# Delta rule on Trainium2: keys multiply the state inside the recurrence, with projections and Gram products between its steps

## The chip, the cores and the metric

The kernel runs on one core of a Trainium2 chip (trn2). TensorE (PE) multiplies, VectorE (DVE) and ScalarE (ACT) work on tiles, GpSimd (POOL) fills tiles, SyncE (SP) issues the transfers. The metric is the device time in microseconds of one execution; less is better. All data is fp32.

## The reference, cut to what matters

The kernel computes four stages in a row: a gated mixer, a mixture of experts, a gated delta rule and an attention over selected tokens. The change is in the third. For every element (B = 8 sequences of T = 512 tokens, H = 8 heads, keys of 128, values of 64) the reference walks the tokens with a state of 64 x 128 for each head:

```python
q, k, v = conv_silu(x @ Wq), conv_silu(x @ Wk), conv_silu(x @ Wv)
q, k = l2norm(q), l2norm(k)
def step(state, inp):
    q_t, k_t, v_t, a_t, b_t = inp
    retained = einsum('bhvk,bhk->bhv', state, k_t)
    state = a_t * (state - b_t * outer(retained, k_t)) + b_t * outer(v_t, k_t)
    return state, einsum('bhvk,bhk->bhv', state, q_t)
out = out * rsqrt(mean(out ** 2) + 1e-5) * o_norm_w * silu(x @ Wg)
y = x + out.reshape(T, 512) @ Wo
```

## The kernel before, in words

`stage_delta` treats the 512 tokens of an element in NC = 4 chunks of 128. Inside a chunk the walk over tokens becomes the inverse of a triangular 128 x 128 matrix for each head, so that all is matrix products, and only the state goes from chunk to chunk (the recurrence).

For an element b, PE does in this order (names of the code in brackets): 8 key projections (`proj`, L1378); the recurrence of the element before it, pb (`scan`, L1392 to L1411); for each chunk the Gram products keys x keys (`gram_kk`, L1422); 4 value projections; the key transposes (`k_transposes`, L1431); 8 query and 4 gate projections; the output transposes and output projection of pb (`project_out`, L1442, L1447); the inversion of b's blocks from 32 to 64 to 128 rows (`invert`: L1463, L1469, L1480, L1485, L1492 for two chunks, then for the other two); at the end of each of the two halves of `invert` the products of scaled keys with the inverse (L1500), which give WT, "the keys already multiplied"; then in `tail` the value transposes (L1509), the products keys x queries (L1518) and the query norms (products with a column of ones, L1523).

In `scan` each chunk has five groups of 8 head products: XT x values and, added in the same bank, WT x state, which give U; queries x state; keys x decayed U, which gives the next state (not for the last chunk); PQ x U, the output. DVE and ACT stand between them: ACT copies U (`u`, L1592), DVE decays state and U (L1743, L1747), adds the new state (L1752) and the output (L1756, L1761). Between these DVE does the causal convolutions (`conv`, three operations each, L1735) and the decay scans (L1765). After the Gram products DVE multiplies them by the decays (L1812), then computes the output's norm (L1816 to L1826) and applies it and the gate (L1828, L1830: semaphore `yf`), then inverts the 32 x 32 diagonal blocks of b by substitution (L1838 to L1858), then adds the residual (L1863, semaphore `outr`), for which `invert` waits. In `invert` DVE scales what PE produced (L1872, L1880) between the convolutions of values and queries.

Every engine runs its own program in a fixed order and waits on semaphores. The first element and the last recurrence are written out, the seven steps between are a hardware loop:

```python
body(None, 0)
with pe.Fori(0, BATCH - 1) as pb:
    body(pb, pb + 1)
body(BATCH - 1, None)
```

## Time and profile before

| | us |
|---|---|
| median of 3 runs (3804.80 to 3806.32) | 3805.78 |
| the profiled execution | 3808.81 |
| its span, first to last instruction | 3806.2 |
| mean granted TensorE clock | 0.864 |

The page gives each engine's busy share over all four stages, so it says little on one of them. The delta rule stage is read from the timeline (instructions of one engine in order of time, merged where they repeat, with the idle time before them and what ended it) and from the busy time by stretch, which also gives the clock that was granted to TensorE: 1.00 is 2.4 GHz and 0.50 is 1.2 GHz, and a value between is a stretch that saw both. A matmul's end is modelled: the start of the next instruction is the safer mark.

### The profile page before, as it was taken

Reading aid. Unit: us, or ns where it says so; the run is one execution under the profiler, and the core shown is the slowest. Engines: PE = TensorE matmul, PEld = TensorE weight load, DVE = VectorE, ACT = ScalarE, POOL = GpSimd, SP = SyncE. Lnnn points to the kernel's source line nnn. Section 1 sums busy time; section 2 is a strip of 40 time slices with the busy share of each in tenths; the row PEclk is TensorE's granted clock in tenths of the full one; section 3 lists DMA queues with packets and bytes.
Section 4 is the critical chain, followed back from the end, with each engine's and each line's share of the span. In section 5 each row is a group of like instructions: output and inputs, shape, how many; then the busy total and the mean of one; then the engine's idle time right before and its main releaser. Section 6 shows DMA issues by size and latency. Waiting matters only on the chain. (4 is left out here: it accounts for less than half of the span.)

```text
span 3806.2 us, 52445 instructions
## 1 busy us (share of the span) xinstructions
PE 3262.9 (86%) x18666; PEld 2525.1 (66%) x18666; DVE 2396.6 (63%) x5801; ACT 1356.5 (36%) x2713; POOL 158.4 (4%) x158
## 2 busy tenths in 40 slices
PE   5999938888999999747989898989898989488887
PEld 2665524445999999714867686868686869355554
DVE  6788425554777777766685858576767673354542
ACT  2333202221444444314534444444444442033232
POOL 0000000015111111000000000000000000000000
PEclk8999958999999999968797988888888886588786
DMA  1000080022899989741011111110111100100000
GB/s 62 23 17 12 11 160 12 11 75 81 305 322 317 320 318 323 253 152 64 34 34 35 34 36 34 35 34 35 34 35 34 35 20 1 53 12 23 12 17 12
DMA packets 203686, 327.31 MB, mean 86 GB/s; under 512 B 37449, under 2 KB 157522, under 8 KB 202258
## 3 DMA queue, kind: packets, MB, share of 16 engines
q1 hardware_dynamic: 196930, 305.94, 24.4%
q0 software_dynamic: 6480, 17.77, 1.2%
q8 instruction: 164, 2.69, 0.3%
q14 instruction: 112, 0.92, 0.1%
HBM read 275.15 MB, written 48.50 MB: 85 GB/s over the span
## 5 line engine op out<-in xcount | busy, mean ns | idle before, releaser
L767 PE MATMUL ex_ps<-ex_xbT,ex_w 128*128 128x128 f32 x4544 | 531.2, 275 | 1.7 <-DMA ex_b<-in_b_all_dram 1.2
L767 PEld LDWEIGHTS ex_ps<-ex_xbT,ex_w 128*128 128x128 f32 x4544 | 524.3, 192 | 6.1 <-DMA ex_b<-in_b_all_dram 1.8
L1378 PE MATMUL de_ps<-de_hT,de_w 128*128 128x512 f32 x640 | 306.2, 636 | 27.6 <-DMA de_w<-in_w_kqv_dram 13.9
L896 ACT ACTIVATE ex_t<-ex_ps,ex_b 128x128 f32<-128x128 f32 x568 | 208.8, 368 | 337.0 <-PE ex_ps L767 319.1
L1378 PEld LDWEIGHTS de_ps<-de_hT,de_w 128*128 128x128 f32 x640 | 129.0, 207 | 188.1 <-issue 186.0
L711 PE MATMUL ex_ps<-ex_xT,ex_w 128*128 128x512 f32 x512 | 230.6, 607 | 12.5 <-DVE ex_gl L1008 9.1
L1008 DVE SCALAR_TENSOR_TENSOR ex_gl<-ex_ps,ex_b,ex_t 128x128 f32<-128x128 f32 (+1 forms) x316 | 123.7, 391 | 137.3 <-ACT ex_t L896 69.4
L711 PEld LDWEIGHTS ex_ps<-ex_xT,ex_w 128*128 128x128 f32 x512 | 98.0, 195 | 131.8 <-issue 115.0
L1735 DVE SCALAR_TENSOR_TENSOR de_ya<-de_kx,de_taps,de_ya 128x512 f32<-128x512 f32 x192 | 142.5, 751 | 49.2 <-ACT de_ya L1574 44.7
L1008 DVE SCALAR_TENSOR_TENSOR ex_gm<-ex_ps,ex_b,ex_t 128x128 f32<-128x128 f32 (+1 forms) x316 | 121.8, 385 | 48.9 <-ACT ex_t L869 46.6
L177 PE MATMUL mx_ps<-mx_hT,mx_w_in 128*128 128x512 f32 x320 | 143.6, 605 | 8.3 <-ACT mx_hT L249 8.3
L1735 DVE SCALAR_TENSOR_TENSOR de_ya<-de_qx,de_taps,de_ya 128x512 f32<-128x512 f32 x192 | 142.9, 751 | 8.7 <-ACT de_ya L1574 2.6
L779 PE MATMUL ex_ps<-ex_w,ex_hid 128*128 128x256 f32 x568 | 134.5, 380 | 1.8 <-DVE ex_hid L1033 1.8
L1485 PE MATMUL de_ps<-de_PQ,de_DG 64*128 64x64 f32 x512 | 113.4, 419 | 15.7 <-ACT de_PQ L1638 15.7
L1485 PEld LDWEIGHTS de_ps<-de_PQ,de_DG 64*128 64x128 f32 x512 | 110.4, 329 | 19.6 <-ACT de_PQ L1638 19.6
L869 ACT ACTIVATE ex_t<-ex_ps,ex_b 128x512 f32<-128x512 f32 x64 | 44.0, 687 | 207.3 <-PE ex_ps L711 207.3
L177 PEld LDWEIGHTS mx_ps<-mx_hT,mx_w_in 128*128 128x128 f32 x320 | 60.7, 193 | 81.6 <-issue 67.4
L211 PE MATMUL mx_ps<-mx_h2T,mx_w_fc 128*128 128x512 f32 x256 | 113.7, 603 | 0.8 <-ACT mx_h2T L271 0.8
L1030 DVE SCALAR_TENSOR_TENSOR ex_gl<-ex_gl,ex_gm 128x128 f32<-128x128 f32 (+1 forms) x316 | 105.4, 333 | 11.1 <-DVE ex_gl L1028 0.2
L1033 DVE TENSOR_TENSOR ex_hid<-ex_gl,ex_gs 128x128 f32<-128x128 f32 (+1 forms) x316 | 105.0, 332 | 11.2 <-DVE ex_gl L1030 0.2
L220 PE MATMUL mx_ps<-mx_w_proj,mx_hid 128*128 128x256 f32 x512 | 111.8, 379 | 0.0
L779 PEld LDWEIGHTS ex_ps<-ex_w,ex_hid 128*128 128x128 f32 x568 | 102.5, 190 | 12.9 <-DVE ex_hid L1033 1.9
(378 smaller groups left out, 6268.3 us busy)
## 6 DMA issues: line engine op xcount, KB each, us to landing
ex_w<-in_w_all_dram SPq DMA_DIRECT2D x144, 1024.0 KB, 6.5
ex_w<-in_w_all_dram SPq DMA_DIRECT2D x72, 512.0 KB, 8.6
de_w<-in_w_kqv_dram SPq DMA_DIRECT2D x80, 256.0 KB, 2.8
de_ab<-alpha_d SPq DMA_DIRECT2D x8, 2048.0 KB, 8.3
ex_xb<-ex_xs_d SPq DMA_DIRECT2D x71, 129.0 KB
ex_xs_d<-ex_blank SPq DMA_DIRECT2D x71, 128.5 KB, 8.3
ex_w<-ex_y_d SPq DMA_DIRECT2D x16, 512.0 KB, 6.1
mx_xin<-in_x_dram SPq DMA_DIRECT2D x8, 512.0 KB, 4.0
```

The source lines that it names most:

```text
L177: m = pe.matmul(ps[:, (n + 2) % 4, :], w_in[:, k, part * DIM + half * P:part * DIM + (half + 1) * P], hT[:, k, :], start=(k == 0), stop=(k ...
L211: m = pe.matmul(ps[:, 4 + f % 2, :], w_fc[:, k, f * P:(f + 1) * P], h2T[:, k, :], start=(k == 0), stop=(k == KT - 1))
L220: m = pe.matmul(ps[:, 6 + t // 2, t % 2 * DIM:(t % 2 + 1) * DIM], hid[:, f, t * P:(t + 1) * P], w_proj[:, f, :], start=(f == 0), stop=(f = ...
L711: m = pe.matmul(ps[:, bank, :], w[:, k, part * HID + c * P:part * HID + (c + 1) * P], xT[:, i % (LAG + 1), k, :], start=(k == 0), stop=(k ...
L767: m = pe.matmul(ps[:, n % 4, x * BLK:(x + 1) * BLK], w[:, k, part * HID + c * P:part * HID + (c + 1) * P], xbT[sx][:, k, :], start=(k == 0 ...
L779: m = pe.matmul(ps[:, 4 + sx, t * DIM:(t + 1) * DIM], hid[:, sx, c, t * P:(t + 1) * P], w2[s][:, c, :], start=(c == 0), stop=(c == HT - 1))
L896: act.activation(t1[:, n % 2, 0:BLK], ps[:, n % 4, 0:BLK], ACT.Identity, bias=b13[s][:, 0, n:n + 1]).then_inc(t1_ready, 1)
L1008: dve.scalar_tensor_tensor(out=out[:, 0:width], in0=in0, scalar=b3[:, 1, n:n + 1], in1=t1[:, n % 2, 0:width], op0=ALU.add, op1=ALU.mult).t ...
L1030: link2(dve.scalar_tensor_tensor(out=gl[:, 0:width], in0=gl[:, 0:width], scalar=1.0, in1=gm[:, 0:width], op0=ALU.add, op1=ALU.mult))
L1378: m = pe.matmul(ps[:, n % 2, :], w[:, g % SLOTS, k, n % 2 * P:(n % 2 + 1) * P], hT[:, k, :], start=(k == 0), stop=(k == KT - 1))
L1485: m = pe.matmul(ps[:, 2 + c % 2, hd * HALF:(hd + 1) * HALF], DG[0:HALF, c, hd, :], X11[0:HALF, c % 2, hd, :], start=True, stop=True, skip_ ...
L1735: m = dve.scalar_tensor_tensor(out=ya[:, n % 3, :], in0=xp(n)[:, i:i + SEQ], scalar=taps[:, col_of(n), i:i + 1], in1=ya[:, n % 3, :], op0= ...
```

## The change

`WT` and its products (L1500) are gone, with ACT's scalings of the keys (L1614) and copies of the result (L1646). In the recurrence the convolved keys multiply the state (`with_state`), DVE scales that and adds it to the values (`add_state`), and only then XT multiplies the sum (`u_products`). For the first chunk, whose state is zero, there are no products with the state: `first_state` and `first_out` are copies. The 4 value projections and the 4 Gram groups of b stand between the steps of pb's recurrence. The keys have two buffers, so that b's can be projected while pb's are used. The squares of the output go from DVE to ACT, the query norm to the start of DVE's part, the loop is written out (`for pb, b in steps`), the residual is loaded into the output tile once that has been transposed, and `Xc` shares the value tile, so that POOL fills it with zeros for each element.

```diff
         PQ = sb("PQ", [P, NC, H, C])
...
         Y5 = sb("Y5", [P, 2, H, HALF])
         tmp = th[:, 0, :]
...
+        squared = lambda t: spare[:, (1 + t // 2 * 2) * Q * Q + t % 2 * VD:(1 + t // 2 * 2) * Q * Q + (t % 2 + 1) * VD]
...
-            def scan(pb):
...
-                pe.wait_ge(s["wt"], pb * NC + NC)
-                for c in range(NC):
-                    bank = 2 + c % 2
+            def scan(pb, b):
+                def u_products(c):
                     for hd in range(H):
-                        pe.matmul(ps[:, bank, hd * V:(hd + 1) * V], XT[:, c, hd, :], vb[:, c, hd, :],
-                                  start=(hd == 0), stop=False, skip_group_check=True)
-                    pe.wait_ge(s["st"], pb * NC + c + 1)
+                        m = pe.matmul(ps[:, 2, hd * V:(hd + 1) * V], XT[:, c, hd, :], vb[:, c, hd, :], start=True, stop=True, skip_group_check=True)
+                    m.then_inc(s["up"], 1)
...
+                def with_state(c):
...
-                        m = pe.matmul(ps[:, bank, hd * V:(hd + 1) * V], WT[:, c, hd, :], ST[:, hd, :],
-                                      start=False, stop=True, skip_group_check=True)
-                    m.then_inc(s["up"], 1)
-                    if c:
-                        pe.wait_ge(s["od"], pb * NC + c)
+                        m = pe.matmul(ps[:, 3, hd * V:(hd + 1) * V], kc(pb, hd, c), ST[:, hd, :], start=True, stop=True, skip_group_check=True)
+                    m.then_inc(s["ks"], 1)
...
-                    if c < NC - 1:
...
+                    pe.wait_ge(s["vs"], pb * (NC - 1) + c)
+
+                def state_step(c):
+                    pe.wait_ge(s["ud"], pb * (NC - 1) + c + 1)
+                    for hd in range(H):
+                        m = pe.matmul(ps[:, 3, hd * V:(hd + 1) * V], kt[:, c, hd, :], Ud[:, hd, :], start=True, stop=True, skip_group_check=True)
+                    m.then_inc(s["su"], 1)
+
...
+                pe.wait_ge(s["pq"], pb * NC + NC)
+                pe.wait_ge(s["vbr"], pb * NC + NC)
+                u_products(0)
+                value(0)
+                state_step(0), outputs(0)
+                value(1)
+                with_state(1), u_products(1)
+                value(2)
+                state_step(1), outputs(1)
+                value(3)
+                with_state(2), u_products(2)
+                if b is not None:
+                    gram_kk(pb, b, 0)
+                state_step(2), outputs(2)
+                if b is not None:
+                    gram_kk(pb, b, 1)
+                with_state(3), u_products(3)
+                if b is not None:
+                    gram_kk(pb, b, 2)
+                outputs(3)
+                if b is not None:
+                    gram_kk(pb, b, 3)
...
-                    pe.wait_ge(s["dg"], b * NC + min(NC, c + 3))
...
                         if p:
-                            pe.wait_ge(s["wt"], b * NC + 2)
+                            pe.wait_ge(s["y6"], b * NC + c - 1)
...
-                    for c in both:
-                        pe.wait_ge(s["x6"], b * NC + c + 1)
-                        pe.wait_ge(s["kcg"], b * NC + c + 1)
-                        bank = 6 if c % 2 == 0 else 2
-                        for hd in range(H):
-                            m = pe.matmul(wide(bank)[:, hd, :], kcg[:, c % 2, hd, :], XT[:, c, hd, :], start=True, stop=True, skip_group_check=True)
-                        m.then_inc(s["wp"], 1)
...
-                pe.wait_ge(s["wt"], b * NC + NC)
                 pe.wait_ge(s["vbr"], b * NC + NC)
+                pe.wait_ge(s["x6"], b * NC + NC)
...
-                    scan(pb)
-                if b is not None:
-                    gram_kk(pb, b)
+                    scan(pb, b)
+                else:
                     for n in range(V0, Q0):
-                        proj(b, n, pb is None)
-                    k_transposes(b)
+                        proj(b, n, True)
+                    for c in range(NC):
+                        gram_kk(None, b, c)
+                if b is not None:
+                    k_transposes(pb, b)
...
-                    step(2, 7), step(3, 7), step(4, 7)
-                u(0)
-                if b is not None:
-                    step(5, 7), step(6, 7)
-                u(1)
-                if b is not None:
-                    step(7, 7)
-                u(2), u(3)
-                if b is not None:
-                    cp(8), cp(9)
+                    step(2, 7), step(3, 7), step(4, 7), step(5, 7)
+                    u(0)
+                    cp(8)
+                    step(6, 7), step(7, 7)
+                    cp(9)
+                    u(1)
+                    cp(10), cp(11)
+                    tap(8), tap(9)
+                    u(2)
+                    squares(0), squares(1)
                     diagonals(0)
-                    cp(10), cp(11)
+                    u(3)
+                    squares(2), squares(3)
                     diagonals(1)
-                    tap(8), tap(9)
                     for c in range(NC):
                         k_out(c)
                     for n in range(Q0, PROJ):
                         cp(n)
-                        if n == 15:
-                            scaled_k(0)
-                    scaled_k(1)
...
-                        step(n + 3, CONV - 1)
-                        w_out(2 * p), w_out(2 * p + 1)
-                        step(n + 4, CONV - 1)
-                        if p == 0:
-                            scaled_k(2)
-                        step(n + 5, CONV - 1)
-                        if p == 0:
-                            scaled_k(3)
+                        step(n + 3, CONV - 1), step(n + 4, CONV - 1), step(n + 5, CONV - 1)
...
+            for pb, b in steps:
+                body(pb, b)
...
+            for b in range(BATCH):
+                if b:
+                    pool.wait_ge(s["up"], (b - 1) * NC + NC)
+                pool.memset(Xc, 0.0).then_inc(s["xz"], 1)
...
+                def first_state():
+                    dve.wait_ge(s["su"], pb * (NC - 1) + 1)
+                    dve.tensor_copy(ST, heads(3)).then_inc(s["st"], 1)
...
+                def add_state(c):
+                    dve.wait_ge(s["ks"], pb * (NC - 1) + c)
+                    dve.wait_ge(s["scl"], pb + 1)
+                    cB(dve.tensor_tensor(KV[:, :, :], heads(3), over_v(ncg[:, pb % 2, c, :]), ALU.mult))
+                    dve.tensor_tensor(vb[:, c, :, :], vb[:, c, :, :], KV[:, :, :], ALU.add).then_inc(s["vs"], 1)
...
+                def first_out():
+                    if pb:
+                        dve.wait_ge(s["out_st"], 16 * pb)
+                    dve.wait_ge(s["os"], pb * NC + 1)
+                    dve.tensor_copy(o[:, 0, :, :], heads(5)).then_inc(s["od"], 1)
...
-                    dve.memset(ST, 0.0).then_inc(s["st"], 1)
...
-                        cD(dve.tensor_tensor(oT[:, t, :].rearrange("p (h v) -> p h v", v=V), o[:, t, :, :], o[:, t, :, :], ALU.mult))
-                        cD(dve.tensor_reduce(om[:, t, :], oT[:, t, :].rearrange("p (h v) -> p h v", v=V), AX.X, ALU.add), wait=(t == TT - 1))
+
+                def sum_squares(t):
+                    dve.wait_ge(s["sqo"], pb * TT + t + 1)
+                    cD(dve.tensor_reduce(om[:, t, :], squared(t).rearrange("p (h v) -> p h v", v=V), AX.X, ALU.add), wait=(t == TT - 1))
...
+                        query_norm()
+                        for n in range(6):
+                            conv(n)
+                        dve.wait_ge(s["cl_ld"], 32 * pb + 32)
+                        decay_u(0)
+                        conv(6)
+                        first_state()
+                        conv(7)
+                        first_out()
+                        decay_state(1)
+                        dve.wait_ge(s["ab_ld"], 16 * b + 16)
+                        decay(0, 1)
+                        add_state(1)
+                        decay(1, 2)
+                        out_a(1)
+                        decay_u(1)
+                        decay(2, 4)
+                        new_state(1)
+                        decay(4, 5)
+                        out_b(1)
+                        decay_state(2)
+                        decay(5, 6)
+                        add_state(2)
+                        decay(6, 7)
+                        out_a(2)
+                        decay_u(2)
+                        decay(7, H)
+                        decayed_gram(0)
+                        new_state(2)
+                        out_b(2)
+                        sum_squares(0), sum_squares(1)
+                        decayed_gram(1)
+                        add_state(3)
+                        out_a(3)
+                        decayed_gram(2)
+                        out_b(3)
+                        cB.end()
+                        decayed_gram(3)
+                        sum_squares(2), sum_squares(3)
+                        normalise()
+
```

## Rows read from the trace of the kernel before

**Rows 1.** The page: busy time, share of the span and instructions of each engine.
```profile
PE 3262.9 (86%) x18666; PEld 2525.1 (66%) x18666; DVE 2396.6 (63%) x5801; ACT 1356.5 (36%) x2713; POOL 158.4 (4%) x158
```

**Rows 2.** Busy time by stretch: length; PE, PEld, DVE, ACT, POOL busy; clock; DMA share; GB/s.
```profile
1985.00:3115.00 1130.00, 1018.07 (x6240) 832.38 (x6240) 788.44 (x1447) 499.13 (x902) 0.00 (x0) 0.85 0.11 35
```

**Rows 3.** Timeline of PE: start, length in us, line, tiles, count [idle before <-releaser].
```profile
1713.16 12.78 PE L1378 MATMUL de_ps<-de_hT,de_w 128*128 128x512 f32 x24 [13.94 <-DMA de_w<-in_w_kqv_dram]
1801.27 7.06 PE L1463 MATMUL de_ps<-de_Xc,de_DG 128*128 128x64 f32 x32 [7.77 <-ACT de_Xc L1620]
1876.90 13.98 PE L1378 MATMUL de_ps<-de_hT,de_w 128*128 128x512 f32 x32
2063.53 6.95 PE L1378 MATMUL de_ps<-de_hT,de_w 128*128 128x512 f32 x9 [1.87 <-issue]
2178.24 3.78 PE L1463 MATMUL de_ps<-de_Xc,de_DG 128*128 128x64 f32 x32 [1.63 <-DVE de_xin L1863]
2197.84 5.98 PE L1500 MATMUL de_ps<-de_XT,de_kcg 128*128 128x128 f32 x32
2204.93 3.79 PE L1463 MATMUL de_ps<-de_Xc,de_DG 128*128 128x64 f32 x32 [1.11 <-ACT de_DG L1646]
2234.81 2.02 PE L1518 MATMUL de_ps<-de_qx,de_kx 128*128 128x128 f32 x16 [0.87 <-DVE de_vb L1892]
2250.99 16.96 PE L1378 MATMUL de_ps<-de_hT,de_w 128*128 128x512 f32 x32 [1.75 <-issue]
2303.36 7.38 PE L1422 MATMUL de_ps<-de_kx 128*128 128x128 f32 x64 [0.96 <-DVE de_o L1761]
2323.32 3.65 PE L1431 MATMUL de_ps<-de_ident,de_kx 128*128 128x128 f32 x16 [3.97 <-ACT de_kt L1596]
3187.74 2.69 PE L1392 MATMUL de_ps<-de_vb,de_XT 128*128 128x64 f32 x16
```

**Rows 4.** Timeline of DVE, same columns.
```profile
2124.32 0.17 DVE L1816 TENSOR_SCALAR de_th<-de_nq 128x32 f32<-128x32 f32 x1
2132.61 0.19 DVE L1822 TENSOR_TENSOR de_th<-de_th 128x32 f32<-128x32 f32 x1
2140.93 2.12 DVE L1838 STREAM_TRANSPOSE de_PQ<-de_PQ 128x1024 f32<-128x1024 f32 x1
2176.75 1.22 DVE L1863 TENSOR_TENSOR de_xin<-de_xin,de_ps 128x1024 f32<-128x1024 f32 x1 [1.54 <-PE de_ps L1447]
2223.02 6.96 DVE L1735 SCALAR_TENSOR_TENSOR de_ya<-de_qx,de_taps,de_ya 128x512 f32<-128x512 f32 x9
2273.19 2.32 DVE L1735 SCALAR_TENSOR_TENSOR de_ya<-de_kx,de_taps,de_ya 128x512 f32<-128x512 f32 x3
3282.88 1.22 DVE L1863 TENSOR_TENSOR de_xin<-de_xin,de_ps 128x1024 f32<-128x1024 f32 x1 [13.55 <-PE de_ps L1447]
```

**Rows 5.** Busy time by stretch: length, PE busy (instructions), granted clock, DMA share, GB/s.
```profile
1741.40:1745.00 3.60, 3.52 (x16) 0.50 0.00 0
1745.00:1748.70 3.70, 1.97 (x18) 1.00 0.00 0
1801.20:1814.60 13.40, 12.58 (x80) 0.50 0.01 1
1814.60:1825.20 10.60, 10.59 (x64) 0.50 0.01 2
1832.60:1839.00 6.40, 5.84 (x64) 1.00 0.00 0
2234.80:2249.30 14.50, 14.42 (x128) 1.00 0.01 2
2267.80:2303.30 35.50, 34.46 (x305) 1.00 0.03 9
3190.30:3251.90 61.60, 61.58 (x289) 0.50 0.00 1
3251.90:3269.40 17.50, 0.01 (x1) 0.50 0.00 0
```

## What I expect of the change, before seeing it run

> **What bounds the kernel now.** I read the page first: TensorE is busy for 86% of 3806.2 us [rows 1], but the page averages four stages. The busy time by stretch puts the middle of the delta rule stage at 1130 us with PE busy for 1018 and the granted clock at 0.85 [rows 2]. So I laid that stage out by the timeline of PE, then of DVE. The stage runs from the first key projection at 1713.2 us to the last residual addition at 3284.1 (1571 us). It has one opening part, 1713.2 to 1876.9 (163.7 us), seven middle steps, 1876.9 to 3187.7 (1310.8 us, 187.3 each), in each of which the recurrence of one element meets the projections and inversion of the next, and a last part of 96.4 us [rows 3, 4].
>
> One middle step, counted from its first key projection, has three stretches [rows 3]. A: projections, recurrence, Gram products, output projection, up to the first product of the inversion (2063.53 to 2178.24, 114.7 us). B: inversion, up to the first key-query product (2178.24 to 2234.81, 56.6). C: key-query and norm products and the loop's branch (2234.81 to 2250.99, 16.2). Two facts decide what the change is worth.
>
> First, A is PE's only up to the Gram products. Then DVE takes over: the output's normalisation ends at 2141.0, at once the inversion of the diagonal blocks runs until 2175.2, the residual is added at 2176.75 (behind 1.54 of waiting), and only then PE may start L1463 [rows 3, 4]. PE's work on the way has slack against this.
>
> Second, the clock. PE runs at 1.00 (2.4 GHz) or 0.50 (1.2 GHz). In the opening part it started L1463 at 0.50 after an idle time of 7.77 us [rows 3], stayed at 0.50 through L1463, L1469, L1480, L1485 and L1492 (24.0 us), and came back only behind the dense 128 x 128 x 128 products of L1500 [rows 5]. After L1500 the products of C run at 1.00. In the last part there is no projection before the recurrence: the 64-column groups run at 0.50 for 61.6 us and never bring the clock back, though PE has no pause [rows 5]. In the middle steps the same groups run at 1.00 behind the projections [rows 5].
>
> **The change part by part.** I lay one middle step out anew, t = 0 at its first key projection.
>
> Loop gone. Six of seven steps now start behind a branch: PE waits 1.75 to 1.87 us with no releaser but issue, and the eight key projections take 16.8 us to the next group's start where the unrolled entry took 13.8 (16.96 and 13.98 in the rows) [rows 3]. Straight code takes the 1.75 away in every step. The other 3.0 is the low clock, and it stays if C ends at 0.50; I keep 16.8 (bounds 13.8 to 16.8).
>
> Recurrence. Per step 19 groups of 16 products become 17 (the state's first two products and the second XT-side product pair are gone for chunk 0; WT x state becomes keys x state). A group costs 34.46 / 19 = 1.8 us, and PE waited for 1.0 in the whole stretch [rows 5]. Four value projections of 13.8 / 8 = 1.72 and four Gram groups of 1.8 move in between, and were on PE's path before, so they cost nothing new. New is a wait: PE does U(0) and one value projection, 16.8 + 3.5 = 20.3, and then needs the decayed U, which DVE now issues behind conv(5). In the old timeline conv(5) starts two 0.6 us operations later than it now can, at 2273.19, and takes 2.3 [rows 4]: 2250.99 + 24.0 is when the new one lands. PE idles 3.8 us. An idle time of 3.97 us stands before the second half of the key transposes, which then take 3.65 us, that is half clock [rows 3]; so two 64-column groups and part of a value projection run low: 3.2 us more, bounds 0 and 5.0. The new pair on DVE that scales keys x state and adds it (two operations of 0.69) is covered by the query group of 1.79 that PE runs meanwhile; if one decay scan of 1.1 is ahead of it, up to 1.1 shows, three times. I take 0. The rest of PE's line is 16 groups, 3 projections and 4 Gram groups: 28.8 + 5.2 + 7.2 = 41.2. The last Gram group ends at 24.1 + 41.2 + 3.2 = 68.5. Before, it started at 2303.36 and ran 7.2 us [rows 3], so it ended 59.6 us into the step.
>
> Normalisation. The 13 small operations on the query norm (from 2124.32, 0.2 us each and their gaps, some 2.9) move to the start, where DVE waits for taps, and the four squares move to ACT, beside PE's groups. Behind the last Gram group remain 0.3 + 1.1 (decayed Gram), 1.2 (two reductions) and 8.4 (2132.61 to 2140.93 and a little) [rows 4]: ready at 79.5. Before it was 77.5. So what left DVE is used up by the Gram products coming 8.9 later. Inversion 34.3 and addition 1.2 follow: L1463 may start at 115.1. Stretch A: 114.7 before, 115.1 after. The queue entries moved here are SP's load of the residual (behind the output transposes, 3.9 us to land, needed 15 us later; SP only has the store behind it) and POOL's fill of the shared Xc tile (after the last U, some 45 us before it is used): nothing. ACT's four value copies now stand between the U copies and are 0.6 each; nothing.
>
> PE meanwhile ends the output projection near 107, some 7 us before 115.1, as in the opening part. So B starts at 0.50.
>
> Inversion. The 64 dense products of L1500 per element are gone (5.98 us in the first half [rows 3], about as much in the second, and 1.1 of waiting between them and the next half's start at 2204.9: 12.8 in all) as are ACT's 32 scalings and 4 copies. But with L1500 goes what brought the clock back. Two halves of 24.0 us at 0.50 lie end to end: 48.0 [rows 5]. DVE ends later: its last three convolutions (7.0) follow the second Y6 at 45.3, end at 52.1, and the value transposes and scalings with their hand-overs take 3.7. First key-query product at 56.0. Stretch B: 56.6 before, 56.0 after. The 12.8 us taken out buy 0.6.
>
> Stretch C. Nothing in it is changed, yet it now begins at 0.50. Its eight groups (four of 128-column products, four of one-column ones, each bound by loading its weights) took 14.5 us at 1.00 [rows 5]. At 0.50 sixteen such products take 3.41 us, as the 289 in 61.6 us of the last part show [rows 5]: 27.3. Stretch C: 16.2 before, 27.3 after.
>
> Sum: 115.1 + 56.0 + 27.3 = 198.4 per step; seven give 1388.8 against 1310.8, so +78.0. The opening part loses 12.8 us of L1500 and up to 7.8 of waiting (the diagonal copies no longer stand behind value copies on ACT) and pays 13 in C: I take 0, bounds -13 and +3. The last part: two groups at 0.50 less (-6.8), 17.5 us of idle PE [rows 5] become 10.6, and new hand-overs with nothing between (U to its decay, 1.0 each, four times) cost 4.1, with the output products slower: about -8. In all +70. The profiled execution took 3808.8 us, its span 3806.2; it becomes 3879. The median of the runs lies 3.0 below the profiled one, so 3876.
>
> A rule that bears on the recurrence: the Trainium skill, "TensorE: Matmul & The Clock Gate", section "A second HAM failure mode: psum-queue depth-cycling", says that many short idle times between groups of products make the clock swing between its two levels. The old recurrence, with waits below 1.1 us between groups, ran at 1.00 throughout, so this trace doesn't bear it out for short waits. Taken at its word it is the third rival.
>
> **Rivals.** (1) The clock comes back in C. Its first key-query group is as dense as L1500's, and two such groups, the Gram products at 1741, began at 0.50 and were followed by 1.00 [rows 5]; against it, each dense group is followed by an equal time of one-column products, and nothing in the trace shows this mix started at 0.50. If it returns behind the first group, C takes 3.4 + 12.6 = 16.0 and the next projections 13.8: the step is 115.1 - 3.0 + 56.0 + 16.0 = 184.1, seven save 22, the opening part 11, the last 8: 3765, or up to 3795 where it fails in two or three steps. This is the case on the other side, faster; it decides on where in C the clock turns.
> (2) It comes back in every second or third step only: 3 to 4 steps at 184 to 188, the rest at 198: 3815 to 3845.
> (3) The low clock after the 3.8 us wait stays through the recurrence, as it did in the last part. Then some 20 groups more run at 0.50, 34 us in each such step. For it speaks that 64-column groups don't lift it; against it the value projection of full width that stands third. One such step gives 3909, two to five 3940 to 4050.
> (4) The change doesn't do what it says: the clock behaves in B as before although PE idled 7 us. Then B keeps 44 to 56, C 14.5, and a step is 170 to 183: 3670 to 3755. The opening part speaks against it.
> (5) Gains and losses cancel, 3798 to 3813: a mixture of (1) and (2).
>
> **How the numbers follow.** Forecast, including one step of (3) at most: 3850 to 3915, chance 0.47. (1) and (4) 0.12, (2) 0.14, (3) with more steps 0.22, (5) 0.05. The range takes in the forecast, (2), (5), the dearer edge of (1), and (3) up to two steps: 3795 to 3955. Within 0.2% (7.6 us, about what a measurement of this kernel can tell from no change) only (5) falls: 0.05. Faster 0.12, slower 0.83.
>
> **What would show it.** Right: PE idle for 3 to 4 us before the first keys x U group of each step; the gap before the first inversion product near 7 us; the granted clock at 0.50 from there through L1492 of both halves; the key-query stretch at 27 us; steps of 198. Wrong: a key-query stretch at 1.00, an inversion that starts earlier than 112 us into the step, or a recurrence at 1.00 throughout.

## The result, and the profile after

The changed kernel takes 3837.39 us (median of 4 runs, 3835.62 to 3847.45) against 3805.29 for the kernel before in the same comparison: a ratio of 1.0091, 95% interval 1.0073 to 1.0109. It is slower by 32 us. I had forecast +70 (3876), so the direction was right and the size was more than twice the real one. The profiled execution spans 3836.0 us, 29.8 more than the one of before.

The busy times of the page move little, against [rows 1]: PE lost 768 instructions and is still busy 30 us longer, and ACT lost 84 us of work.

```profile
PE 3293.1 (86%) x17898; PEld 2559.0 (67%) x17898; DVE 2394.9 (62%) x5793; ACT 1272.0 (33%) x2457; POOL 171.1 (4%) x165
```

Where the 29.8 us come from is seen when each step is a stretch of its own. The columns are those of [rows 2]: length; PE, PEld, DVE, ACT, POOL busy; clock; DMA share; GB/s. The first row is the opening part (without its first 1.3 us), the others the seven middle steps.

```profile
1713.00:1865.50 152.50, 125.91 (x623) 95.68 (x623) 103.19 (x177) 66.66 (x107) 0.00 (x0) 0.74 0.09 32
1865.50:2050.10 184.60, 164.79 (x946) 135.45 (x945) 131.20 (x240) 72.33 (x118) 1.80 (x1) 0.80 0.11 35
2050.20:2234.60 184.40, 164.62 (x946) 135.61 (x946) 131.13 (x240) 72.33 (x118) 1.80 (x1) 0.80 0.11 35
2234.60:2430.80 196.20, 176.33 (x947) 147.34 (x946) 131.20 (x240) 72.33 (x118) 1.80 (x1) 0.75 0.11 35
2430.80:2629.50 198.70, 178.68 (x945) 148.39 (x946) 131.21 (x240) 72.32 (x118) 1.80 (x1) 0.73 0.10 33
2629.50:2827.60 198.10, 178.05 (x945) 148.22 (x946) 131.15 (x240) 72.33 (x118) 1.80 (x1) 0.73 0.10 33
2827.60:3025.70 198.10, 177.99 (x946) 148.19 (x946) 131.19 (x240) 72.33 (x118) 1.80 (x1) 0.73 0.10 33
3025.70:3223.70 198.00, 177.87 (x946) 148.11 (x946) 131.19 (x240) 72.32 (x118) 1.80 (x1) 0.73 0.07 25
```

All seven steps hold the same work (945 to 947 matmul instructions, the same DVE and ACT time to 0.1 us), yet there are two lengths. The last four take the forecast's 198 us. The first two take 184.5, and the third lies between. Against the 187.3 us of before, the seven together cost +47.3 (1358.2 against 1310.8). The opening part, 153.8 us from its first projection against 163.7 [rows 3], gives back 9.9. The last part, from 3223.7 to the last residual addition at 3313.1, gives back 6.9. The stage begins 1.5 earlier, and what follows it takes 0.8 longer: in all +29.8.

What separates the two lengths is the clock of the key-query stretch. The timeline of PE (columns of [rows 3]) for the third element and then for the fourth, each from the second pair of value transposes on:

```profile
2216.14 1.97 PE L1531 MATMUL de_ps<-de_ident,de_vx 128*128 128x128 f32 x8 [3.00 <-DVE de_vb L1952]
2218.94 3.40 PE L1540 MATMUL de_ps<-de_qx,de_kx 128*128 128x128 f32 x16 [0.83 <-issue]
2222.17 1.84 PE L1545 MATMUL de_ps<-de_ones,de_ya 128*128 128x1 f32 x16
2223.88 2.03 PE L1540 MATMUL de_ps<-de_qx,de_kx 128*128 128x128 f32 x16
...
2234.60 13.98 PE L1376 MATMUL de_ps<-de_hT,de_w 128*128 128x512 f32 x32
```

```profile
2400.67 1.97 PE L1531 MATMUL de_ps<-de_ident,de_vx 128*128 128x128 f32 x8 [3.00 <-DVE de_vb L1952]
2403.47 3.75 PE L1540 MATMUL de_ps<-de_qx,de_kx 128*128 128x128 f32 x16 [0.83 <-issue]
2407.01 3.41 PE L1545 MATMUL de_ps<-de_ones,de_ya 128*128 128x1 f32 x16
2410.29 3.76 PE L1540 MATMUL de_ps<-de_qx,de_kx 128*128 128x128 f32 x16
...
2430.77 17.00 PE L1376 MATMUL de_ps<-de_hT,de_w 128*128 128x512 f32 x32
```

Both come out of the inversion at 0.50, with the same pauses of 3.00 and 0.83 us, and their first key-query group begins at 0.50. In the upper one the clock turns near that group's end: the next group takes 1.84, and so on at 1.00. In the lower one it doesn't: the whole stretch runs at 0.50, and so do the first 6 us of the next projections (0.51 from 2430.8 to 2437.0, then 1.00), which take 17.00 instead of 13.98. By stretch:

```profile
2219.00:2234.60 15.60, 15.60 (x129) 15.60 (x129) 4.90 (x4) 3.15 (x5) 0.00 (x0) 0.91 0.01 1
2403.50:2430.80 27.30, 27.30 (x129) 27.30 (x129) 4.90 (x4) 3.15 (x5) 0.00 (x0) 0.50 0.04 10
```

The first three of the eight stretches came back (16.0, 15.7 and 15.6 us), the other five took 27.3 each. The rest of a step is as it was laid out:

```profile
2255.59 3.37 PE L1403 MATMUL de_ps<-de_oT,de_kt 128*128 128x64 f32 x16 [3.51 <-DVE de_oT L1760]
2258.76 3.62 PE L1409 MATMUL de_ps<-de_oT,de_PQ 128*128 128x64 f32 x16
2262.17 3.73 PE L1376 MATMUL de_ps<-de_hT,de_w 128*128 128x512 f32 x4
2265.69 2.14 PE L1392 MATMUL de_ps<-de_oT,de_kx 128*128 128x64 f32 x16
...
2347.75 7.06 PE L1492 MATMUL de_ps<-de_vb,de_DG 128*128 128x64 f32 x32 [6.70 <-DVE de_o L1921]
```

```profile
2347.80:2371.70 23.90, 23.08 (x144) 22.33 (x144) 12.45 (x19) 10.21 (x17) 0.00 (x0) 0.50 0.25 80
2371.70:2395.70 24.00, 23.18 (x146) 22.41 (x145) 16.45 (x25) 10.97 (x20) 0.00 (x0) 0.50 0.00 1
```

The wait for the decayed U is there (3.51), two groups and the value projection behind it run at 0.50 and then the clock is back, PE is idle 6.70 us before the inversion, and the two inversion halves take 24 us each at 0.50 throughout. Before, the second half was followed by dense products at L1500 and the key-query products ran at 1.00 [rows 3, 5].

### The profile page after: what moved, and what is told of

Read it like the earlier page. It is cut to its first block and busy times, and to the rows that moved or that the text cites. A ratio compares the mean times of both kernels' runs of the same rounds, so it can differ in the third digit from the quotient of the medians.

```text
span 3836.0 us, 48336 instructions
## 1 busy us (share of the span) xinstructions
PE 3293.1 (86%) x17898; PEld 2559.0 (67%) x17898; DVE 2394.9 (62%) x5793; ACT 1272.0 (33%) x2457; POOL 171.1 (4%) x165
## 5 line engine op out<-in xcount | busy, mean ns | idle before, releaser
L1376 PE MATMUL de_ps<-de_hT,de_w 128*128 128x512 f32 x640 | 312.0, 642 | 19.2 <-DMA de_w<-in_w_kqv_dram 13.8
L1492 PE MATMUL de_ps<-de_vb,de_DG 128*128 128x64 f32 x512 | 113.2, 422 | 56.9 <-DVE de_o L1921 47.6
L1492 PEld LDWEIGHTS de_ps<-de_vb,de_DG 128*128 128x128 f32 x512 | 110.4, 332 | 61.2 <-issue 60.3
L1956 DVE TENSOR_TENSOR de_PQ<-de_ps,de_ab 128x1024 f32<-128x1024 f32 x32 | 39.2, 1225 | 135.0 <-PE de_ps L1540 135.0
```

The costliest lines, as they stand in the source:

```text
L1376: m = pe.matmul(ps[:, n % 2, :], w[:, g % SLOTS, k, n % 2 * P:(n % 2 + 1) * P], hT[:, k, :], start=(k == 0), stop=(k == KT - 1))
L1492: m = pe.matmul(ps[:, 2 + c % 2, hd * HALF:(hd + 1) * HALF], DG[:, c, hd, :], Xc[:, c * H + hd, :], start=True, stop=True, skip_group_chec ...
```

## The experiments

The theory: all that the change takes away, and more, goes to the clock. The dense products of L1500 had brought it back. Without them only the first key-query group can, and whether it does hangs on the moment at which it falls. The rivals: something the first elements do differently, the waits of the new order, or the loop.

**1. The old kernel, its loop written out.** It isolates the loop, the part of the change that has nothing to do with the order of work.

```diff
...
-            body(None, 0)
-            with pe.Fori(0, BATCH - 1) as pb:
-                body(pb, pb + 1)
-            body(BATCH - 1, None)
+            for pb, b in steps:
+                body(pb, b)
```

> The kernel before with its hardware loop written out, nothing else. In the kernel before, six of its seven middle steps begin with 1.75 to 1.87 us of idle PE and with a clock at 0.50 for the first projections (16.8 us for eight instead of 13.8); the one step that is written out takes 186.6 by 13.8. Theory (the branch costs its idle time, and through that idle time the clock at the start of the next step): 4.7 to 6.3 us per step for six steps, so 3768 to 3778. Rival (a step's length is set by DVE's chain, and what PE gains at the start is waited for later): 3795 to 3806.

Measured: 3783.39, ratio 0.9931 (0.9915 to 0.9948): 26 us faster than the kernel before in this comparison (3809.43), 22 against the 3805.29 above. The idle time and the slow projections are both gone (the eight take 13.98 again), so the price of the branch is real. But six steps became 184.3 to 184.4, not 181 to 183; one took 180.8. The first inversion half tells why. It takes 26.7 us in the old kernel's loop [rows 3] and 30.5 here:

```profile
2537.65 6.51 PE L1462 MATMUL de_ps<-de_Xc,de_DG 128*128 128x64 f32 x32 [3.29 <-DVE de_xin L1858]
2544.09 3.62 PE L1468 MATMUL de_ps<-de_PQ,de_Y 128*64 128x32 f32 x32
```

PE arrives earlier, waits 3.29 us instead of 1.63 [rows 3], and enters the inversion with the clock falling. Part of what straight code gave at the front was paid back there. The change therefore has to be held against 3783, and its new order of work costs some 54 us, not 32 (58 if each is held against the kernel before in its own comparison, 52 by the spans of the two traces).

**2. The old kernel with thin products at L1500.** Same count, place and waits; only 32 of the 128 rows are contracted. (The timeline counts each of these fp32 products twice: a group of eight in the code is x16. L1500 has four such groups per element: 32 products in the code, 64 in the timeline. The text below speaks of 64 groups and means these.)

```diff
-                            m = pe.matmul(wide(bank)[:, hd, :], kcg[:, c % 2, hd, :], XT[:, c, hd, :], start=True, stop=True, skip_group_check=True)
+                            m = pe.matmul(wide(bank)[:, hd, :], kcg[0:Q, c % 2, hd, :], XT[0:Q, c, hd, :], start=True, stop=True, skip_group_check=True)
```

> The kernel before with its 64 groups of products at L1500 contracted over 32 of the 128 rows (the result of these products is therefore not the reference's). Their count, their place and all waits stay. Theory (the dense products of L1500 brought the clock back to 1.00 for what follows, and that is what the change lost): the first half's L1500 no longer brings 1.00, the second half of the inversion and the key-query products run at 0.50, a step takes 12 to 16 us more than 187.3, the kernel 3880 to 3915. Rival (the clock comes back by the key-query products or the transposes in any case, and L1500 is only time): within 5 us of 3806, and key-query products at 1.00.

Measured: 3896.54, 87 us slower, as the theory said. L1500 and what follows it, in the third middle step:

```profile
2409.76 6.82 PE L1500 MATMUL de_ps<-de_XT,de_kcg 32*128 32x128 f32 x31
2417.68 7.09 PE L1463 MATMUL de_ps<-de_Xc,de_DG 128*128 128x64 f32 x32 [1.11 <-ACT de_DG L1646]
```

In the old kernel these rows are 5.98 and 3.79 us [rows 3]. The second inversion half ran at 0.50 in all eight elements, and three of the eight key-query stretches stayed at 0.50 from end to end; the other five came back, without a pattern that their work explains. In four of these five the clock was back before the key-query products began, behind the value transposes, which follow the thin products without a pause:

```profile
1864.78 3.50 PE L1509 MATMUL de_ps<-de_ident,de_vx 128*128 128x128 f32 x16
1869.26 2.02 PE L1518 MATMUL de_ps<-de_qx,de_kx 128*128 128x128 f32 x16 [0.98 <-DVE de_vb L1892]
```

So the key-query group is not the only one that can turn the clock; in the changed kernel the value transposes stand between pauses of PE. What L1500 did for the clock was worth 87 us here. The rival that the clock returns in any case falls for the inversion; for the key-query stretch it holds in some elements and not in others, as in the changed kernel.

**3. Eight dense products in front of the key-query products.** In the changed kernel:

```diff
                 pe.wait_ge(s["x6"], b * NC + NC)
+                for i in range(8):
+                    pe.matmul(ps[:, i // 4 % 2, i % 4 * P:(i % 4 + 1) * P], kc(b, i % H, 0), kc(b, i % H, 0), start=True, stop=True, skip_group_check=True)
                 for c in range(NC):
```

> The changed kernel with 8 more products of 128 x 128 x 128 just before the first key-query group of each element (into a bank that is free; their result is not used). In the changed kernel the key-query stretch takes 14.8 to 15.2 us where its clock came back and 25.6 where it did not (five of eight). Theory (whether the first dense group lasts long enough at 0.50 to turn the clock is a matter of tenths of a us, and the cost is all in this): all eight stretches at 1.00 behind the added products, all steps 184 to 187, the kernel 3763 to 3785. Rival (the norm products between the groups pull the clock down again, whatever stands ahead): key-query stretch 20 to 27, kernel 3836 to 3855.

Measured: 3797.26, ratio 0.9968 (0.9957 to 0.9980). (By the rows above the two lengths of the stretch are 15.6 to 16.0 and 27.3 us, longer than that text has them.) All eight stretches came back and the two lengths of step are gone, six of the seven steps being 187.5 to 187.7. The mechanism held; the size was off by 12 us because the added products and most of the first key-query group still ran at 0.50:

```profile
2413.40 3.76 PE L1537 MATMUL de_ps<-de_kx 128*128 128x128 f32 x16 [0.83 <-issue]
2416.95 3.06 PE L1542 MATMUL de_ps<-de_qx,de_kx 128*128 128x128 f32 x16
2419.85 1.84 PE L1547 MATMUL de_ps<-de_ones,de_ya 128*128 128x1 f32 x16
```

The one-column products between the dense groups, which I had held against a return, don't pull the clock down again once it is back.

**4. The decay of the first U ahead of the sixth convolution.** In the changed kernel:

```diff
-                        for n in range(6):
+                        for n in range(5):
                             conv(n)
                         dve.wait_ge(s["cl_ld"], 32 * pb + 32)
                         decay_u(0)
+                        conv(5)
                         conv(6)
```

> The changed kernel with DVE's decay of the first U ahead of its sixth key convolution, as the kernel before had it. It takes away the 3.7 us for which PE waits before the first keys x U group. Theory (that stretch is the processor of the recurrence alone; the step's end hangs on DVE's normalisation and inversion chain, which gains little): the wait falls below 1.6 us, the recurrence stays at 1.00 from its start, the inversion begins 0.5 to 1.5 us earlier in a step, and the kernel is 0 to 10 us faster beside what the key-query stretch does (3826 to 3837 with the same three of eight at 1.00; up to 3870 where fewer come back). Rival (the wait and the low clock behind it are on the path in full): 5 to 7 us per step, 3787 to 3801.

Measured: 3841.20. PE's wait before keys x U fell to 1.28 us, but a new one of 1.99 for ACT stands one group later, because ACT still copies U behind the activation of the convolution that DVE now does later:

```profile
2465.88 2.00 PE L1403 MATMUL de_ps<-de_oT,de_kt 128*128 128x64 f32 x16 [1.28 <-DVE de_oT L1760]
2469.87 3.68 PE L1409 MATMUL de_ps<-de_oT,de_PQ 128*128 128x64 f32 x16 [1.99 <-ACT de_oT L1614]
```

Against steps of the same clock at both ends, it saves 0.1 to 2.5 us (193.7 to 193.9 against 196.2 where a step starts at 1.00 and ends at 0.50; 197.0 to 197.9 against 198.0 to 198.7 where both are 0.50). The kernel as a whole gained nothing, because two of its eight key-query stretches came back, not three. The 3.8 us wait is a real but small term.

**5 and 6. A delay, once.** The changed kernel, with one (then three) multiplications more on DVE in the first element alone. Nothing in the later elements differs.

```diff
                     dve.wait_ge(s["dd"], 2 * b + 2)
+                    if first:
+                        for c in range(1):
+                            dve.tensor_tensor(o[:, c, :, :].rearrange("p h v -> p (h v)"), ident4[:, :, :].rearrange("p h t -> p (h t)"), ident4[:, :, :].rearrange("p h t -> p (h t)"), ALU.mult)
```

> The changed kernel with one DVE multiplication of 128x512 (0.6 to 0.7 us) more in the inversion of the first element alone; it delays everything behind it once. Theory (whether a key-query stretch comes back to 1.00 is decided by where its first dense group falls in time, to some tenths of a us, and a delay of 0.6 us moves some of the three stretches that came back out of that place): one or two of eight come back instead of three, each lost one costs 10 to 14 us, the kernel 3846 to 3866; it may also move another in, so what is measured is first of all another number or another set of stretches at 1.00. Rival (the first elements differ from the later ones by something they do, the filling of a queue or a transfer): the same first three stretches at 1.00 and 3838.

> As before it, with three such multiplications (1.9 to 2.1 us of delay). Theory of the place in time: none of the first three stretches comes back, the kernel 3860 to 3880 (all eight at 0.50 is what the prediction on record put at 3876); if the first value projection too falls badly behind the wait of 3.8 us, one recurrence stays at 0.50 for 34 us more. Rival (something in the first elements): the same three stretches, 3839.

Measured: 3851.83 (3838.82 to 3866.70) with one, 3877.16 (3873.55 to 3883.07) with three, ratio 1.0177 (1.0160 to 1.0194). With one delay the profiled execution brought the clock back in the first stretch only:

```profile
1851.70:1867.40 15.70, 15.69 (x129) 15.70 (x129) 4.91 (x5) 3.15 (x5) 0.00 (x0) 0.91 0.00 1
2036.30:2063.50 27.20, 27.20 (x128) 27.20 (x129) 4.90 (x4) 3.15 (x5) 0.00 (x0) 0.50 0.04 10
```

With three, in none. Here is the first stretch, which in the changed kernel took 16.0 us; the seven steps behind it take 197.9 to 198.1 each:

```profile
1852.40:1879.70 27.30, 27.30 (x129) 27.30 (x129) 4.90 (x4) 3.15 (x5) 0.00 (x0) 0.50 0.04 14
```

The first inversion started 83.7 us into the stage with three (82.3 with one) against 82.0 without: a delay of 1.7 us in one place cost 40 (38.5 by the spans of the traces, 35 if each kernel is held against the kernel before in its own comparison). This rules out that the first three elements do something that the others don't, and it is the direct evidence for the place in time. What the place is measured against, no run here shows. A part of the shift isn't mine: the stage began at 1711.7, 1713.7 and 1713.0 us in the three profiled executions. That may also be why the runs of experiment 5 spread over 28 us; it was not shown. The medians of experiment 6 and of the changed kernel lie further apart than either's runs. No recurrence of a middle step stayed at 0.50 in any of these kernels.

**7. Ten dense products where PE waits for DVE.** In the changed kernel, between the second and the third value transposes:

```diff
                     m.then_inc(s["vtp"], 1)
+                    if c == 1:
+                        for i in range(10):
+                            pe.matmul(ps[:, i // 4 % 2, i % 4 * P:(i % 4 + 1) * P], kc(b, i % H, 0), kc(b, i % H, 0), start=True, stop=True, skip_group_check=True)
```

> The changed kernel with 10 more products of 128 x 128 x 128 per element between the second and the third group of value transposes, where PE waits 3.0 us for DVE in any case (2.1 us of work at 1.00, 4.3 at 0.50; results not used). Theory (it takes dense work ahead of the key-query products, and there it costs less than the 8 products right in front of them, which added 3.4 us): the key-query stretch begins at 1.00 and takes 13.5 to 14.5, steps of 183 to 186, the kernel 3765 to 3785. Rival (a pause of 0.8 us and the transposes behind it undo it): as the changed kernel or worse, 3825 to 3860.

Measured: 3745.07, ratio 0.9825 (0.9808 to 0.9841), steps of 180.7 to 182.2, 20 us better than the better end of what I expected. The clock is back before the key-query products, not in their midst:

```profile
2572.42 2.86 PE L1535 MATMUL de_ps<-de_kx 128*128 128x128 f32 x20
2575.62 1.25 PE L1531 MATMUL de_ps<-de_ident,de_vx 128*128 128x128 f32 x8 [0.34 <-DVE de_vb L1955]
2577.70 2.02 PE L1543 MATMUL de_ps<-de_qx,de_kx 128*128 128x128 f32 x16 [0.83 <-issue]
```

With eighty more dense products this kernel is 92 us faster than the changed one.

**8 and 9. The clock held ahead of the inversion too, and the delay again.** The edit of experiment 4; 28 dense products behind the output projection, in the 6.70 us of idle PE; 8 behind the last inversion product of an element. Experiment 9 adds the delay of experiment 6.

```diff
             def invert(pb, b):
                 pe.wait_ge(s["ktr"], b * NC + NC)
+                pe.wait_ge(s["cp"], b * PROJ + PROJ)
+                for i in range(28):
+                    pe.matmul(ps[:, i // 4 % 2, i % 4 * P:(i % 4 + 1) * P], kc(b, i % H, 0), kc(b, i % H, 0), start=True, stop=True, skip_group_check=True)
...
                         m.then_inc(s["x6p"], 1)
+                    for i in range((0, 8)[p]):
+                        pe.matmul(ps[:, i // 4 % 2, i % 4 * P:(i % 4 + 1) * P], kc(b, i % H, 0), kc(b, i % H, 0), start=True, stop=True, skip_group_check=True)
```

> The changed kernel with three edits. DVE decays the first U ahead of the sixth key convolution; 28 dense products run behind the output projection, where PE is idle for 7 us before the inversion; 8 dense products stand behind each element's last inversion product (results of the added ones not used). Theory (all that the change lost is in the granted clock: the idle time ahead of the inversion puts its first half at 0.50, as nothing did before the change, and the missing L1500 keeps the rest there): the first inversion half begins at 1.00 and takes 19 to 21 us instead of 24, the key-query stretch runs at 1.00, steps of 177 to 181, the kernel 3715 to 3745, faster than the kernel before. Rival (DVE and ACT set the inversion's length, whatever the clock): steps of 184 to 187, 3775 to 3800.

> The changed kernel with the three edits that gave 3719.5 (the decay of the first U ahead of the sixth convolution, 28 dense products ahead of the inversion, 8 behind its last product) and the once-only delay of about 2 us in the first element which, in the changed kernel without these edits, took it from 3837.4 to 3877.2. Theory (with enough dense work the clock no longer hangs on where groups fall in time): 3719 to 3727, all eight key-query stretches at 1.00, steps of 177.5. Rival (the three edits only hit a lucky place in time, as the first three elements of the changed kernel did): some stretches at 0.50, 3735 to 3800.

Measured: 3719.45, ratio 0.9755 (0.9739 to 0.9771), steps of 177.5 to 177.9, the first inversion half 19.6 us in all seven. With the delay 3723.08 (3719.81 to 3726.32), all eight stretches at 1.00: the medians differ by 3.6 us here where they differed by 40, and the runs of the two overlap (3713.10 to 3722.43 without the delay); the spans differ by 0.2. With this much dense work ahead, the same delay no longer decides anything.

**10. The clock held in the old order.** Experiment 1, with 12 such products between output projection and inversion (the first edit of experiment 8 with 12 for 28).

> The kernel before with its loop written out (3783.4) and 12 dense products in the 3.3 us for which PE waits between output projection and inversion; L1500 and the rest of the old order stay. It asks what the changed order is worth where the clock is held in both. Theory (the old order too pays for the low clock in the first inversion half, 3.7 us per step, and gets it back here; what then remains between it and 3719.5 is the changed order's own gain, mostly L1500's 12 us): first inversion half 26 to 27.5 us instead of 30.5, steps of 180 to 182, the kernel 3752 to 3768. Rival (the changed order has no gain of its own, all is the clock): 3715 to 3740.

Measured: 3768.57, ratio 0.9892 (0.9876 to 0.9909), 0.6 above the theory's range; in the seven steps the first inversion half takes 25.9 to 26.9 us again, and a step 180.7 to 181.3, the first 184.4. With dense products added to both, the changed order (3716.42, experiment 12, which has the edit of experiment 4 too) is 52 us faster than the old one. By their traces, 53.0 us of span: 14.6 in the opening part, 27.2 in the seven steps, 7.8 in the last part and behind it, and 3.4 ahead of the stage, where the two kernels are the same. The comparison is not quite even: in five of the seven steps of the old order PE ran part of the output projection at 0.50 and came late to the inversion (no wait before it, 110.6 to 114.3 us into the step against 109.7 to 109.8 in the other two). Of the seven steps' gain some 5 us may be this. The rest shows that the change does save time on the path; as it stood, the clock hid it.

**11. Real work in place of added products.** The changed kernel with the edit of experiment 4 and the four gate projections moved into the inversion, two behind each half:

```diff
                     k_transposes(pb, b)
-                    for n in range(Q0, PROJ):
+                    for n in range(Q0, G0):
...
                         m.then_inc(s["x6p"], 1)
+                    proj(b, G0 + 2 * p, False), proj(b, G0 + 2 * p + 1, False)
...
                         step(n + 3, CONV - 1), step(n + 4, CONV - 1), step(n + 5, CONV - 1)
+                        cp(G0 + 2 * p), cp(G0 + 2 * p + 1)
```

> The changed kernel, no product added: the four gate projections (full-width products that are needed only in the next step) go from ahead of the output projection into the inversion, two behind each half's last product, with ACT's gate activations behind them; and the decay of the first U ahead of the sixth convolution. Theory (real dense work can do what the added products did: two projections behind each half bring the clock back; the 6.9 us lie in the inversion, where PE is on the path for part of it): key-query stretches at 1.00, steps of 180 to 186, the kernel 3740 to 3785. Rival (moved into the inversion, the projections add their 6.9 us to the path, up to 13.7 at 0.50, and PE's longer idle time ahead of it costs more): steps above 190, 3800 to 3850.

Measured: 3769.65, ratio 0.9901 (0.9884 to 0.9919). The clock is back behind each half and the key-query stretch runs at 1.00, but the two pairs take 5.86 and 5.22 us between the inversion's products, and PE waits 13.46 us before the inversion:

```profile
2529.11 7.06 PE L1492 MATMUL de_ps<-de_vb,de_DG 128*128 128x64 f32 x32 [13.46 <-DVE de_o L1924]
...
2553.07 5.86 PE L1380 MATMUL de_ps<-de_w_g,de_hT 128*128 128x512 f32 x8
```

It beats the kernel before (3808.05 in this comparison) by 38 us without a single product whose result is not used, and the old order with its loop written out (3783.39, another comparison) by some 14.

**12. The best version.** Experiment 8 with the 8 products behind the inversion replaced by the 10 of experiment 7.

> As the kernel that gave 3719.5, but with the 8 dense products behind the last inversion product replaced by 10 between the second and third value transposes, where PE waits for DVE. Theory (it only matters that the clock is back by the first key-query group, and behind the inversion DVE is what is late): the same steps within 1 us, 3712 to 3728. Rival (the filler behind the inversion delays the value transposes and so the key-query products, by up to 3.4 us): steps of 174 to 176, 3690 to 3710.

Measured: 3716.42 (3715.89 to 3717.15), ratio 0.9757 (0.9740 to 0.9773), steps of 177.5 to 177.8 as in experiment 8. One step, its first inversion half, its second, and its key-query stretch:

```profile
2393.40:2570.90 177.50, 165.81 (x1022) 137.16 (x1022) 131.08 (x240) 72.34 (x118) 1.80 (x1) 0.85 0.11 37
2505.10:2524.70 19.60, 17.22 (x142) 16.67 (x143) 12.31 (x20) 10.66 (x17) 0.00 (x0) 0.70 0.31 97
2524.70:2549.00 24.30, 23.48 (x149) 22.72 (x148) 16.75 (x25) 10.97 (x20) 0.00 (x0) 0.50 0.00 1
2556.00:2570.00 14.00, 13.43 (x121) 13.46 (x121) 4.89 (x6) 3.15 (x5) 0.00 (x0) 1.00 0.00 1
```

The second half still runs at 0.50. Whether holding it too would pay was not tried; DVE is busy for 16.75 of its 24.3 us.

## Why the prediction was right and wrong

| step of the prediction | forecast | measured |
|---|---|---|
| wait before the first keys x U group | 3.8 us, and 3.2 for the low clock behind it | 3.51; 4.8 at a start at 1.00 (3.17 + 3.41 + 3.52 against 1.73 + 1.79 + 1.77) |
| last Gram group ends, us into the step | 68.5 | 66.9 (start at 1.00), 68.8 to 69.5 (start at 0.50) |
| PE idle before the inversion | near 7 | 6.70 |
| L1463 (now L1492) starts | 115.1 | 113.1 to 113.2, or 115.0 to 115.7 |
| inversion up to the first key-query product | 56.0, all at 0.50 | 55.7 to 55.8, all at 0.50 |
| key-query stretch | 27.3 in all | 27.3 in five, 15.6 to 16.0 in three |
| a step | 198.4 | 198.0 to 198.7 in four; 184.6, 184.4 and 196.2 |
| opening part | 0 (-13 to +3) | -9.9 |
| last part | -8 | -6.9 |

**The step that failed** is "Stretch C". I wrote that "nothing in the trace shows this mix started at 0.50", and then let one value stand for all eight stretches, as if the clock were a property of the mix. It is not. The same first group turned it in three elements and not in five, and experiments 5 and 6 show that the moment at which it falls decides. Three steps came out 13.8, 14.0 and 2.2 us below 198.4: 30 of the 40 us by which the sum was too high. The opening part is the other 10. I bounded it from -13 to +3 and took 0, and it is the same step that failed there: its key-query stretch was one of those that came back, and cost 1.8 us where I had put 13. The inversion started 6.1 us earlier (82.0 against 88.1 us into it), since ACT's diagonal copies no longer stand behind the value copies: DVE waits 2.61 us for them where it waited 8.94. The inversion itself took 55.7 us instead of 61.3. That makes -9.9. In experiment 6, where this stretch stayed at 0.50, the opening part took 166.7 us, 1.7 of them the delay, which is 1.3 more than before and close to my 0. That 0 was luck all the same: my own three terms (12.8, up to 7.8, and 13) add up to as much as -7.6, and L1500's 12.8 gave only 5.6.

```profile
1759.10 2.08 DVE L1896 STREAM_TRANSPOSE de_PQ<-de_PQ 128x1024 f32<-128x1024 f32 x1 [2.61 <-ACT de_PQ L1626]
```

**What was right.** The path through DVE's normalisation and block inversion, the order of the terms, the exact price of a step whose clock doesn't return (four steps at the forecast's length to 0.4 us), and that the 12.8 us of L1500 buy 0.6 in the inversion (measured 0.8 to 0.9). Experiment 6, with the same work and all eight stretches at 0.50, takes 3877.2 where the forecast's case said 3876 (66.7 above the kernel before in its own comparison, where I had said 70).

**The rivals.** Rival 2 (the clock back in some stretches, 3815 to 3845) held the result; I gave it 0.14 because I looked for a reason why the mix would turn, not for a reason why it would turn always alike. Its pattern was wrong (the first three, not every second or third). Rival 3, a recurrence that stays at 0.50 behind the wait, did not occur in a recurrence that has projections ahead of it, in the changed kernel or an experiment. The Trainium skill's rule that stood beside it ("TensorE: Matmul & The Clock Gate", section "A second HAM failure mode: psum-queue depth-cycling") has thus only this to point to here: waits of 3.51 us put two groups and a projection at 0.50, once per step, and in experiment 4 waits of 1.28 and 1.99 us close to each other did it too (3.68 us for the group behind them). Rival 4 fell: no inversion half of a middle step ran at 1.00.

**The loop.** I took 1.75 us per step for it and kept the 3.0 of slow projections; the idle time is 1.75 to 2.29 us in the six passes, not 1.75 to 1.87. Experiment 1 shows 3.4 us per step in the old order (1286.9 us for the seven steps against 1310.8).

## What to carry to other kernels

Before removing products, ask what they do to the clock as well as what they cost: here 10 added dense products per element, in time when PE was idle anyway, were worth 92 us, and the change that lost 32 us as it stood was some 50 us ahead of the old order once both had dense products added for the clock. Where a stretch starts at 0.50 and its first dense group is all that could turn the clock, forecast a mixture with the steps counted both ways, and add or move dense work until a small delay no longer changes the time.

## What the runs showed of the hardware

- A delay of 1.7 us in one element of eight moved the kernel by 35 to 40 us (3837.4 to 3877.2), through the clock that was granted to the same work. With dense products ahead the same delay moved it by 0 to 4.
- Products of one column between dense groups did not lower the clock once it stood at 1.00 (key-query stretch of experiment 12: 1.00). Where the clock had not turned at the first group, the same mix never turned it: five stretches of 27.3 us in the changed kernel, PE busy throughout, stayed at 0.50 to their end.
- Contracting over 32 rows in place of 128 left the count and the place of L1500's products as they were and took away their effect on the clock: 3896.5 against 3809.4 us.
- Writing the loop out saved 22 to 26 us over six passes. The branch's idle time, 1.75 to 2.29 us a pass, is 12.0 of them; the eight projections behind it took 16.8 instead of 13.8 us, and part of these 3.0 was lost again in the inversion (30.5 instead of 26.7 us for its first half).
